# A decoder layer's cross-attention: queries for eight batches in the first pass, stored and loaded again for the second

## What is computed

```
x = rmsnorm(layernorm(hidden)) * ln_weight
h_q = (x @ w_q.T).reshape(b, lq, H, DH)
h_k = (key_value_states @ w_k.T).reshape(b, lk, H, DH)
h_v = (key_value_states @ w_v.T).reshape(b, lk, H, DH)
score = einsum('bqhd,bkhd->bhqk', h_q, h_k) + position_bias[None]
score = where(m, softmax(where(m, score, -inf)), 0)
attn = einsum('bhqk,bkhd->bqhd', score, h_v).reshape(b, lq, H * DH)
out = attn @ w_out.T
return hidden_states + out
```

## Time and profile before

| | |
|---|---|
| time, median of 3 (lowest to highest) | 916.41 us (914.9 to 916.72) |
| the profiled execution's own time | 916.63 us |
| its span in the trace | 914.8 us |
| busy: PE, DVE, ACT, POOL | 904.4, 697.0, 515.9, 663.8 us |
| instructions on PE (matmuls) | 5150 |
| chain that ended last | PE 87%, DVE 10%, POOL 1%, issue 1% |
| granted TensorE clock, mean | 0.996 |
| DMA, mean over the span | 164 GB/s |

### The profile page before, as it was taken

One profiled execution on the slowest core, in us unless ns is written; L12 is line 12 of the kernel. 1 busy time (PEld: TensorE's weight loads), 2 busy tenths in 40 slices (PEclk: granted clock), 3 DMA queues, 4 the chain that ended last, 5 costly groups with the idle time before them and its releaser, 6 DMA issues.

```text
span 914.8 us, 15425 instructions
## 1 busy us (share of the span) xinstructions
PE 904.4 (99%) x5150; PEld 778.9 (85%) x5150; DVE 697.0 (76%) x763; ACT 515.9 (56%) x1188; POOL 663.8 (73%) x429
## 2 busy tenths in 40 slices
PE   9999999999999998999999999999999999999998
PEld 8687688888888887888899999999899999999876
DVE  5699997999999999456666676676666677767774
ACT  3686868576665675365655555555555555555330
POOL 3247788997678776457698878788878888787522
PEclk9999999999999999999999999999999999999999
DMA  9555476675777753356554444545454545454302
GB/s 310 166 156 166 143 230 184 204 208 183 215 238 229 241 171 126 110 170 226 162 169 157 137 158 135 158 136 158 137 159 135 158 135 160 134 169 136 109 1 93
DMA packets 96849, 150.26 MB, mean 164 GB/s; under 512 B 10576, under 2 KB 35280, under 8 KB 96672
## 3 DMA queue, kind: packets, MB, share of 16 engines
q1 hardware_dynamic: 86432, 131.54, 44.3%
q10 hardware_dynamic: 10368, 18.09, 7.9%
HBM read 113.81 MB, written 35.78 MB: 164 GB/s over the span
## 4 chain that ended last, share of the span: by engine, by line
PE 87%; DVE 10%; POOL 1%; issue 1%; ACT 0%; DVEq 0%; ACTq 0%; POOLq 0%
PE acc L508 11%; PE acc L510 11%; PE acc L509 11%; PE misc L510 6%; PE misc L508 6%; PE misc L509 6%; PE acc L789 6%; PE acc L734 6%; PE acc L666 5%; PE acc L667 5%; PE acc L668 5%; DVE misc L1225 4%; PE acc L758 3%; DVE w L1232 2%; DVE misc L1220 2%
## 5 line engine op out<-in xcount | busy, mean ns | idle before, releaser
L1486 POOL TENSOR_TENSOR y<-y,w 128x2048 f32<-128x2048 f32 x31 | 143.5, 4630 | 58.4 <-DVE w L1232 57.4
L1225 DVE TENSOR_TENSOR_SCAN misc<-dA,misc 128x2048 f32<-128x2048 f32 x32 | 141.7, 4429 | 4.3 <-ACT dA L862 1.1
L1083 ACT ACTIVATE prob<-prob,negm 128x128 f32<-128x128 f32 x256 | 99.9, 391 | 41.6 <-DVE negm L1295 41.6
L1090 ACT ACTIVATE ot_hi<-acc 128x512 fp32r<-128x512 f32 x64 | 38.3, 599 | 143.3 <-PE acc L789 143.3
L1547 POOL TENSOR_TENSOR wt_lo<-ws,wt_hi 128x1024 fp32r<-128x1024 f32 x27 | 65.1, 2410 | 61.7 <-ACT wt_hi L1071 61.7
L508 PE MATMUL misc<-wo_hi,ot_hi 128*128 128x512 f32 x256 | 107.1, 418 | 0.5 <-POOL wo_lo L1564 0.5
L510 PE MATMUL misc<-wo_hi,ot_lo 128*128 128x512 f32 x256 | 101.3, 396 | 0.0
L508 PE MATMUL acc<-wv_hi,ctx_hi 128*128 128x512 f32 x256 | 101.2, 395 | 0.0
L509 PE MATMUL misc<-wo_lo,ot_hi 128*128 128x512 f32 x256 | 100.8, 394 | 0.0
L510 PE MATMUL acc<-wv_hi,ctx_lo 128*128 128x512 f32 x256 | 100.0, 391 | 0.0
L509 PE MATMUL acc<-wv_lo,ctx_hi 128*128 128x512 f32 x256 | 99.9, 390 | 0.0
(11 more groups left out here) (196 smaller groups left out, 2438.6 us busy)
## 6 DMA issues: line engine op xcount, KB each, us to landing
k_scratch<-kst SPq DMA_DIRECT2D x64, 256.0 KB, 3.6
bc<-xp_scratch ACTq DMA_DIRECT2D x32, 512.0 KB, 5.7
v_scratch<-vst SPq DMA_DIRECT2D x32, 512.0 KB, 4.2
k_sb<-k_scratch SPq DMA_DIRECT2D x64, 256.0 KB, 2.9
v_sb<-v_scratch SPq DMA_DIRECT2D x64, 256.0 KB, 2.7
wo_raw<-in_wo SPq DMA_DIRECT2D x64, 256.0 KB, 2.9
wp<-in_wq SPq DMA_DIRECT2D x54, 256.0 KB, 3.8
wraw<-in_wk SPq DMA_DIRECT2D x32, 256.0 KB, 5.0
```

The costliest lines, as they stand in the source:

```text
L1083: last = act.activation(prob[q][:, b], prob[q][:, b], ACT.Exp, bias=negm[q][:, b:b + 1], accum_out=psum[q][:, b:b + 1])
L1225: dve.tensor_tensor_scan(h_ps, flat(dA[k % 2][:, :, :, :]), h_ps, 0.0, ALU.mult, ALU.add).then_inc(da_free, 1)
L1486: pool.tensor_tensor(y_half(half), y_half(half), w[:, k % 2], ALU.add).then_inc(y_ready, 1)
```

## The change

The blocks of the paired scheme are now (two heads) x (two halves of the features) x (batches 0 to 3, batches 4 to 7): each product has 512 columns, and a pair gives the queries of two heads for all eight batches. So pairs exist in the first pass alone: 13 of them, heads 6 to 31 (FIRST_PAIR = 3, PAIRS = 16). The halves for batches 0 to 3 (c11, c21) go to q_sb as before; those for batches 4 to 7 (c12, c22) go to q_st and are stored to q_scratch in memory. Heads 0 to 5 are unpaired in both passes (steps 0 to 5 and 32 to 37). In steps 38 to 63 SyncE loads q_sb[g] from memory, right behind k and bias of the head, and scores are made in step g itself and no longer in g+1 (`scored`); step 38 makes those of heads 37 and 38. PV of the second pass writes psY, not psT. Further: out is split into the 8 matmuls with ot_hi, then the wait for ot_lo and the 4 with it; one V sum of the last group stands ahead of the y transposes, and none behind step 1; the T sums are made by DVE and GpSimd (`t_sums`), rounded on ACT behind step 3; in unpaired steps GpSimd's weight sums stand behind bm and wo_lo; ACT splits the next wq ahead of the queries' copy; the loads and products for the linear layer's weights stand in later steps (H + 4, H + 5, H + 7).

```diff
-FIRST_PAIR = 5
-PAIRS = H
-HALF_T = HT // 2
+FIRST_PAIR = 3
+PAIRS = H // 2
+PLAIN = 2 * FIRST_PAIR
 W11, W12, W22, S1, S2, S3, S4 = range(7)
 T1, T2, T3, T4 = range(4)
-KZ = 12
-Y_AT = KP
+Y_AT = KP + 1
+KZ = KP + 5
...
+        def ps_o(k, half):
+
+            return psY if (k >= H if known(k) else half) else psT
+
         four = [psQ, psS, psY, psT]
-        sumX, sumY = psQ[:, 0:HALF_T], psY[:, 0:HALF_T]
+        sumX, sumY = psQ, psY
...
-            for g in range(H - 4, H + 4):
+            for g in range(H - 4, H + 8):
                 step(g, g, g // H, g // 2)
                 behind(g)
-            with eng.Fori(H // 4 + 1, STEPS // 4 - 1) as i:
+            with eng.Fori(H // 4 + 2, STEPS // 4 - 1) as i:
...
-            return known(g) and g < 2 * FIRST_PAIR
-
-        def paired(i):
-
-            return not known(i) or FIRST_PAIR <= i < PAIRS
+            return known(g) and (g < PLAIN or H <= g < H + PLAIN)
+
+        def nth(g):
+
+            return g if g < H else g - H + PLAIN
+
+        def paired(i, half):
+
+            return FIRST_PAIR <= i < PAIRS if known(i) else half == 0
+
+        def loaded(g, half):
+
+            return H + PLAIN <= g < STEPS if known(g) else half == 1
+
+        def scored(g, half):
+
+            if not known(g):
+                return [(g, 0)] if half else [(g - 1, 1)]
+            return [(k, g - k) for k in (g - 1, g) if runs(k) and loaded(k, half) == (k == g)]
+
+        def q_count(g, p):
+
+            return 8 * (g - p) - 8 * (H + PLAIN) + 16
...
+                if paired(i, half) and p:
+                    sp.wait_ge(c12_done, count(i))
+                    sp.dma_start(q_dram[g - 1], q_st[0][:]).then_inc(q_stored[0], 16)
                 if runs(g) and runs(g + 1):
                     if not known(g) or g >= 1:
                         sp.wait_ge(sb_done, g)
                     load_kb(g + 1, head(g + 1, half), 1 - p)
+                if known(g) and g == H + PLAIN - 1:
+                    for k in range(2):
+                        sp.wait_ge(q_stored[k], 16 * count(PAIRS - 1))
+                if loaded(g + 1, half):
+                    sp.dma_start(q_sb[1 - p][:], q_dram[head(g + 1, half)]).then_inc(q_in[1 - p], 16)
                 if runs(g):
                     if not known(g) or g >= 2:
                         sp.wait_ge(pv_done, g - 1)
                     if not known(g) or g >= 2:
                         sp.wait_ge(wo_lo_done, g - 1)
                     sp.dma_start(wo_raw[p][:], a["wo"][head(g, half)]).then_inc(wo_in[p], 16)
+                if paired(i, half) and p:
+                    sp.wait_ge(c22_done, count(i))
+                    sp.dma_start(q_dram[g], q_st[1][:]).then_inc(q_stored[1], 16)
...
+            v_group(NG - 1, range(1))
             for b in range(HB):
                 pe.wait_ge(y_ready, NSTEP + b)
                 y_transpose(HB + b, misc[:, b]).then_inc(yt_ps, 1)
-            v_group(NG - 1, range(KZ - KP))
+            v_group(NG - 1, range(1, KZ - KP))
...
-            def z_of(half, kc, tok):
-                part = slice(tok * HALF_T, (tok + 1) * HALF_T)
+            def z_of(half, kc):
                 ks = range(kc * C // 2, (kc + 1) * C // 2)
-                return [z_hi[:, half, c, part] for c in ks], [z_lo[:, half, c, part] for c in ks]
-
-            def t_of(half, t):
-                return [tz[half][:, t, 0, c] for c in range(C // 2)], [tz[half][:, t, 1, c] for c in range(C // 2)]
+                return [z_hi[:, half, c] for c in ks], [z_lo[:, half, c] for c in ks]
+
+            def t_of(t):
+                return [tz[t][:, 0, c] for c in range(C // 2)], [tz[t][:, 1, c] for c in range(C // 2)]
...
+                    if g == H:
+                        pe.wait_ge(z_lo_done, 1 + C)
+                        pe.wait_ge(c12_done, count(PAIRS - 1))
...
+                for k, back in scored(g, half):
+                    kp = (p + back) % 2
+                    if plain(k):
+                        pe.wait_ge(q_evac, nth(k) + 1)
+                    elif loaded(k, half):
+                        pe.wait_ge(q_in[kp], q_count(k, kp))
                     elif p:
                         pe.wait_ge(c11_done, count(i))
-                        pe.wait_ge(c12_done, count(i))
                     else:
                         pe.wait_ge(c21_done, count(i) - 1)
-                    pe.wait_ge(kb_in[1 - p], in_count(g - 1, 1 - p, 32))
-                    if not known(g) or g > 1:
-                        pe.wait_ge(sb_done, g - 1)
+                    pe.wait_ge(kb_in[kp], in_count(k, kp, 32))
+                    if not known(k) or k > 0:
+                        pe.wait_ge(sb_done, k)
                     else:
                         pe.wait_ge(dbx_done, NSTEP)
                     for b in range(HB):
-                        mm = pe.matmul(psS[:, b * S:(b + 1) * S], q_sb[1 - p][:, b * S:(b + 1) * S],
-                                       k_sb[1 - p][:, b * S:(b + 1) * S], start=True, stop=True)
+                        mm = pe.matmul(psS[:, b * S:(b + 1) * S], q_sb[kp][:, b * S:(b + 1) * S],
+                                       k_sb[kp][:, b * S:(b + 1) * S], start=True, stop=True)
                     mm.then_inc(s_done, 1)
...
-                    pe.wait_ge(ot_lo_done, g - 2)
+                    pe.wait_ge(ot_hi_done, g - 2)
                     pe.wait_ge(wo_lo_done, g - 2)
                     for b in range(HB):
                         tok = slice(b * S, (b + 1) * S)
                         if known(g) and g - 3 == H:
                             pe.wait_ge(x2_done, b + 1)
-                        mm = three(misc[:, b], ot_hi[q][:, tok], ot_lo[q][:, tok], wo_hi[q][:], wo_lo[q][:],
-                                   h == 0, h == H - 1)
+                        pe.matmul(misc[:, b], ot_hi[q][:, tok], wo_hi[q][:], start=h == 0, stop=False)
+                        pe.matmul(misc[:, b], ot_hi[q][:, tok], wo_lo[q][:], start=False, stop=False)
+                    pe.wait_ge(ot_lo_done, g - 2)
+                    for b in range(HB):
+                        tok = slice(b * S, (b + 1) * S)
+                        mm = pe.matmul(misc[:, b], ot_lo[q][:, tok], wo_hi[q][:], start=False, stop=h == H - 1)
                     mm.then_inc(o_done, 1)
...
-                if g == 1:
-                    v_sum(NG - 1, B - 2)
...
+                if plain(g + 1):
+                    split_wq(g + 1, 1 - p)
...
-                    act.activation(q_sb[0][:, 0:HALF_T], sumX, ACT.Copy).then_inc(c11_done, 1)
-                if plain(g + 1):
-                    split_wq(g + 1, 1 - p)
-                if paired(i + 1) and not p:
+                    act.activation(q_sb[0][:], sumX, ACT.Copy).then_inc(c11_done, 1)
...
+                if g == 3:
+                    high_t((T1, T2))
+                    high_t((T3, T4))
...
+                        dve.wait_ge(q_stored[1], 16 * count(i) - 16)
+                    dve.tensor_tensor(q_st[1][:], sumY, q_w[:], ALU.add).then_inc(c22_done, 1)
...
+                        dve.wait_ge(q_stored[0], 16 * count(i) - 16)
+                    dve.tensor_tensor(q_st[0][:], sumX, q_u[:], ALU.add).then_inc(c12_done, 1)
+                elif paired(i, half):
+                    dve.wait_ge(p4_done, count(i))
                     dve.wait_ge(s_done, g - 1)
-                    dve.tensor_tensor(q_sb[0][:, HALF_T:HT], sumX, q_u[:], ALU.add).then_inc(c12_done, 1)
-                elif paired(i):
-                    dve.wait_ge(p4_done, count(i))
-                    dve.tensor_tensor(q_sb[1][:, 0:HALF_T], sumY, q_s1[pp][:], ALU.add).then_inc(c21_done, 1)
+                    dve.tensor_tensor(q_sb[1][:], sumY, q_s1[pp][:], ALU.add).then_inc(c21_done, 1)
...
+            def t_sums():
+                dve.wait_ge(z_lo_done, 1)
+                dve.wait_ge(z_evac, C)
+                for c in range(C):
+                    dve.tensor_tensor(tr[c // 2][:, 0, c % 2], z_hi[:, 0, c].bitcast(F32), z_lo[:, 0, c].bitcast(F32),
+                                      ALU.add).then_inc(z_full, 1)
+                dve.wait_ge(z_full, 2)
+                dve.tensor_tensor(tr[T1][:, 1], z_raw[:, 1, 0:C // 2], tr[0][:, 0], ALU.subtract).then_inc(t12_raw[0], 1)
+                dve.wait_ge(t12_raw[0], 1)
+                dve.tensor_tensor(tr[T2][:, 1], z_raw[:, 1, C // 2:C], tr[T1][:, 1], ALU.subtract).then_inc(t12_raw[1], 1)
...
+                if not plain(g):
+                    pair_sums(g, p, pp, half, i)
...
+                if plain(g):
+                    pair_sums(g, p, pp, half, i)
```

More of the change, by code:

```diff
@@ L199, in decoder_layer @@
         sb(whole, "w0_end", [P, HT - S - 6 * HB - 2 * HB - S // 4])
+        with ExitStack() as sums:
+            q_s1 = [sb(sums, f"q_s1{i}", [P, HT]) for i in pair]
+            q_u = sb(sums, "q_u", [P, HT])
+            q_w = sb(sums, "q_w", [P, HT])
         ea_sb = sb(whole, "ea_sb", [P, ER, D])
@@ L208, in decoder_layer @@
         ffn_w = sb(whole, "ffn_w", [P, C, D])
```

(28 more changed lines are left out.)

234 lines of the change are left out of this document (110 added, 124 removed).

## The result

| | before | after |
|---|---|---|
| median of the timed executions (lowest to highest) | 915.82 us (914.9 to 916.72) | 938.79 us (937.93 to 941.19) |
| ratio, 95% interval | | 1.0247 [1.023, 1.0264] |
| span of the profiled execution | 914.8 us | 936.6 us |

The account below looks back on a forecast made before the run. TensorE, busy 99% of the span, was taken as the bound, a step costing the sum of its pieces. Terms -4.3 - 2.7 + 0.8 + 2.0 + 5.3 + 1.1 + 9.4 = +11.6 on 914.8, plus 1.8, gave 928.2 us, range 911 to 938.

Parts of the forecast that it names:

- Sign: Whole kernel: slower, forecast 928.2 us, with a chance of 0.70 for slower.
- The loaded steps' wait, +9.4: Heads 40 to 63: S waits for q from memory, 23 steps at 0.41 over 4.92; bounds 0 and +18.
- E + 1.94: Loaded steps: forecast issue time of q, fifth in its burst, counted from E, the end of PV of g-2.
- E + 5.6: Loaded steps: forecast landing of q, counted from the end of PV, the lower of two bursts in the trace.
- E + 6.3: Loaded steps: q's landing by the slower burst, counted from the end of PV; upper bound, +18 in all.
- rival 1: Loaded steps: the queries land in time and TensorE's period stays 4.92; 918.8 us, chance 0.24.
- Work, -4.3: Pipeline: wider products change TensorE's sum from 483.8 to 480.8, and a wait of 1.3 in paired steps goes.
- +5.3 for the evacuations: Paired steps: TensorE waits for double-width copies c21 (+0.28) and c11 (+0.13), 13 x 0.41; bounds 0 and 8.
- First pair, +2.0: Before the first W11 product: TensorE stalls for GpSimd's wt_lo, between 0 and 3.0, taken as +2.0.
- Entry, -2.7 and +0.8: Before the pipeline: a V sum fills the 2.9 wait (-2.7); missing behind step 1, it uncovers the first softmax (+0.8).
- Step 38, +1.1: Hand-over: S of heads 37 and 38 in one step, the second needing the first one's bank, +1.1.
- Tail, 0: Last steps: DVE's norm hooks would delay T once by one or two; the last loaded wait was left out for it.

Follow-up runs that it names:

- e1: Changed kernel with k, bias and q of head g+2 issued ahead of SyncE's wait for PV, right behind head g's score sum: 923.21 us, 1.0075.
- e2: Changed kernel with q's loads in the second pass left out, queue order kept, so those queries are missing in the result: 927.45 us, 1.0126.
- e11: Changed kernel with the edits of e1, e4 and e10, ScalarE's T copy for T3 and T4 one step later, and statistics in step 35: 911.98 us, 0.9957.
- e8: Changed kernel with c11 and c21 copying only their first 256 of 512 columns, some queries missing in the result: 934.17 us, 1.0199.
- e10: Changed kernel with two products of a paired step exchanged, W12 ahead of S2, all work done: 934.11 us, 1.0198.
- e7: Kernel before with the change's entry alone: one V sum ahead of the y transposes, one more behind them, none behind step 1: 916.07 us, 0.9991.
- e6: Changed kernel with the edits of e1 and e4, and the third normalization's statistics taken from step 62 to step 39: 925.45 us, 1.0102.
- e3: Changed kernel with the wait for PV kept, but k, bias and q issued ahead of v and wo behind it: 927.75 us, 1.0119.
- e4: Changed kernel with GpSimd's weight sums put ahead of bm and wo_lo again in unpaired steps: 935.35 us, 1.021.

## Why the prediction was right or wrong

**Sign and mechanism: right.** The change saves little of TensorE's work and lets it in for waits, above all for q. Undoing that wait (e1) gives back 15.6 of 23.

**The loaded steps' wait, +9.4: the step that failed, by its size.** It measured +18.0: 131.13 over 23 steps of 4.92. The mechanism, one step in two held up by q, was the forecast's; its loop of 4.92 + 5.74 took 5.08 + 6.33. The stretch was 8.9 over the forecast. Four parts:
- The issue. I put q at E + 1.94, with gaps of 0.37 and 0.48 from a burst in the paired steps and 0.42 for the rest. In the burst shown all four gaps are 0.53 and the first issue is at E + 0.33: E + 2.44. Most steps with a wait have E + 2.3 to 2.5.
- The landing. I took E + 5.6, the lower of two bursts; here q landed at E + 6.07, and S started 0.26 behind it, where I took 0.14 from an engine's result in the earlier trace rows. The two are the 6.33 - 5.74 = 0.59 of a loop, 6.8 over 11.5 loops. Over the steps with a wait the landings spread from E + 5.8 to 6.8, on both sides of my upper bound of E + 6.3; that bound's +18 would have been right for the stretch.
- TensorE's own step. I worked out 4.92 as the unpaired step less its queries. In the changed kernel it is 5.08 where nothing is waited for, 0.16 more in one step of two, 1.8 in all; in e1 it is 5.01. Of that, 0.08 is PV: with S behind it it takes 0.89 (778.61 to 779.50 in e1), where the queries behind it in an unpaired step gave 0.81 (448.79 to 449.60 in the kernel before).
- The last step, which I had taken as covered at the tail: 0.4.

The Trainium skill, "DMA: Bandwidth & Descriptors", section "Anatomy of one DMA", has a fit for GpSimd's path, from which I had estimated 4.5 us for these five transfers. From the first issue at 777.28 to q's landing it was 5.7, so the fit doesn't carry over to this burst of SyncE's, and rival 1 (q in time) fell. In e2, even without q, TensorE waits for bias.

**Work, -4.3 with +5.3 for the evacuations: right in kind, both costs a little too high.** A pair without waits is 19.74 in e11, where I had 19.98: the growth of a product from 256 to 512 columns is (19.74 - 15.04) / 42 = 0.112, not 0.1175, since I took the wider product from twelve in an unpaired step, which have one start behind an fp32 piece among them (0.31 for 0.23), and the narrower from six that have none. By the Trainium skill, "TensorE: Matmul & The Clock Gate", section "Back-to-back issue gap", a pair would grow by 4.5, an estimate from a figure that the page gives for an isolated matmul; it grew by 4.7, between that and my 4.94. The evacuations cost 0.29 a pair (e8, e10), not 0.41. Together 13 x 0.36 = 4.7 less than forecast, which hid part of the other errors.

**First pair, +2.0: too small, and outside its bound of 3.0.** S(4) to S(5) is 14.81, where the same step of a later pair is 9.26: 5.5. I had named the condition (GpSimd left alone by VectorE) and then taken a value in the middle. It wasn't left alone: low_t and the weight sums overlap, and two of them took 3.5 for 1.5, 2.0 of the wait of 3.8. Behind it comes a term I hadn't thought of, the clock: from 421.9 to 425.3 it was 0.50, and from the first W11 product to the second matmul of out TensorE took 3.69, where the same pieces take 2.17 at 1.00 (the products 1.50 in e11, T and a matmul of out 0.67 in an unpaired step): 1.5.

**Entry, -2.7 and +0.8: right in its two terms, but 1.2 too small.** -3.1 for -1.9. The wait for y fell by 2.5, and the first softmax cost 0.7 (S(0) to S(2) fell by 2.06, the V sum taken out by 2.73). The missing term is the clock again. In the kernel before, the wait of 2.9 was followed by this:

```profile
365.40:368.80 3.40, 3.40 (x14) 2.96 (x13) 1.24 (x3) 2.55 (x5) 0.04 (x1) 0.50 0.00 0
```

The sixteen transposes of y and the four matmuls behind them took 4.59 from their first start, and 3.23 in the changed kernel, where the wait is 0.5 and the clock stays at 1.00: 1.4. In e7 it stays up too, and 1.95 of the 3.1 is kept; the rest goes to the wait for wq_lo.

**Step 38, +1.1: near.** TensorE waited 1.2 for DVE's prob there, and S(37) to S(38) was 2.27 for 1.92. The two steps behind it took 5.39 and 6.60, forecast 4.92 and 5.33. I had costed the linear layer's loads, moved behind head 32, at nothing, since their own use is far off; but those of step 37 stand ahead of q of step 39 in SyncE's queue. That is 0.15 in this execution and up to 0.9 in the others (e1). Without such a wait (e2) the step is 5.21; those 0.2 over 5.01 I can't place. In 6.60 TensorE waited 1.3 for q, which landed 4.7 after its issue.

**Tail, 0: wrong by 2.7.** I left out the last wait for q because the hooks there would cover it. They cost more than it, since bm is queued behind the inverse root: e6 and e11, with the statistics elsewhere, take 5.0 for 7.6.

## What to carry to other kernels

When a step gets shorter or a result is wanted a step earlier, list for each load which wait stands ahead of it in the issuing queue, and count from the end of that wait with the slower of the bursts that the trace has; moving the issue ahead of an unrelated wait gave back 15.6 us here. Work hung on a step as filler (statistics, T copies, sums) must be placed by what is queued behind it on every engine that waits for it: the same 2.8 us of statistics cost 2.6 at the tail, 4.0 in step 39 and nothing in step 35. A wait of TensorE can cost more than its length: two of 2.9 and 3.8 us brought 1.4 and 1.5 more through the clock, so look at the granted clock behind each long one. And when a bank is overwritten behind a short piece, look for another product that can go between before making the copy faster.

## What the runs showed of the hardware

- SyncE's DMA issues were 0.53 us apart in the burst of five shown of the second pass, 0.43 to 0.57 in the next one, and 0.37 to 0.48 in a burst of the first; in the steps that waited clearly for q, S started 0.23 to 0.26 us after its landing.
- A load of 256 KB landed, in the median, 3.6 us after its issue both as the fifth of five (after) and as the third of five (e3), and 3.1 when the five were split in two groups 1.8 us apart (e1).
- TensorE's granted clock fell to 0.50 (1.2 GHz) behind waits of 2.9 us (before, 365.4 to 368.8) and 3.8 us (after, 421.9 to 425.3), and stayed at 1.00 behind waits of 1.9 (e4) and 1.7 (e7). In eight of thirteen profiled executions it also fell near 38 us, and everything behind came 1.5 or 3.2 later.
- GpSimd's sum of 256 columns went from 0.73 to 1.7 us beside a VectorE subtraction on 1024 columns in SBUF, and bm in e6 from 1.16 to 2.15; the VectorE instruction itself was also longer beside GpSimd's (two of them 2.88 in the one run, 3.82 in e6).
